# Attention's values multiplied by thirds of a group's rows, and placed by transfers on chip

## The reference

```python
h = jnp.concatenate([tok(x), txt], axis=1)          # 16 x 69 x 256
n = layernorm(h)
q, k, v = n @ wq.T, n @ wk.T, n @ wv.T              # q, k rotated
attn = softmax(einsum('bqd,bkd->bqk', qr, kr) / 16)
h = h + einsum('bqk,bkd->bqd', attn, v)
h = h + shared(n2) + routed_top2_of_8(n2)           # n2 = layernorm(h)
```

## Time and profile before

| | |
|---|---|
| median of 3 runs | 323.93 us (323.28 to 326.38) |
| the profiled execution | 324.18 us, of which the span is 322.0 us |
| busy: PE / DVE / ACT / POOL | 91% / 50% / 45% / 64% of the span |
| granted clock of TensorE, mean | 0.988 of full speed |
| chain that ended last | PE 51%, DVE 17%, DMA 10%, issue 8%, POOL 6%, ACT 4% |
| hardware queue of SP's DMAs (q1) | 14226 packets, 14.03 MB |

### The profile page before, as it was taken

How to read it: one execution, slowest core, us unless ns; L and a number is a source line. 1 busy time by engine, 2 the same in 40 slices (tenths; PEclk the granted TensorE clock), 3 DMA queues, 4 the chain that set the end, 5 groups by cost and what they waited for, 6 DMA issues and landing times.

```text
span 322.0 us, 6614 instructions
## 1 busy us (share of the span) xinstructions
PE 293.1 (91%) x2021; PEld 264.9 (82%) x2022; DVE 161.5 (50%) x414; ACT 144.6 (45%) x325; POOL 206.6 (64%) x168
## 2 busy tenths in 40 slices
PE   0899879898998999998999999999999999999970
PEld 0477878797898999986999989999899998999860
DVE  3777888988837998632233332333323333233220
ACT  3786332558779346524343333433334333343300
POOL 3466490546880007589889889888988897255541
PEclk9999999997999999999999999999999999999997
DMA  7996113024345233865433643632555432324432
GB/s 246 307 214 218 32 46 133 2 70 148 103 175 170 86 115 107 267 227 172 158 89 157 195 128 100 195 109 97 169 164 150 62 49 49 49 32 49 51 37 29
DMA packets 21988, 39.90 MB, mean 124 GB/s; under 512 B 2977, under 2 KB 18290, under 8 KB 19666
## 3 DMA queue, kind: packets, MB, share of 16 engines
q0 software_dynamic: 7456, 25.43, 29.6%
q1 hardware_dynamic: 14226, 14.03, 14.3%
q10 hardware_dynamic: 288, 0.20, 0.2%
HBM read 28.84 MB, written 6.93 MB: 111 GB/s over the span
## 4 chain that ended last, share of the span: by engine, by line
PE 51%; DVE 17%; DMA 10%; issue 8%; POOL 6%; ACT 4%; POOLq 2%; SPq 0%; DVEq 0%; ACTq 0%
PE ps L1007 11%; PE ps L1009 11%; PE ps L1008 11%; DMA out_tokens<-xy_all,dest 8%; PE ps L875 7%; PE ps L1055 4%; PE ps L906 2%; POOL out_tokens L611 2%; POOLq L608 1%; DVE ps L1299 1%; DVE qk L1298 1%; PE ps L977 1%; DVE hid L1415 1%; DMA xp<-in_patches 1%; ACT hn L737 1%
## 5 line engine op out<-in xcount | busy, mean ns | idle before, releaser
L456 POOL TENSOR_TENSOR ring<-stage,ring 128x512 fp32r<-128x512 f32 (+2 forms) x30 | 76.2, 2539 | 2.5
L1604 DVE TENSOR_TENSOR hgT<-ps,hgT 128x512 fp32r<-128x512 f32 x50 | 32.2, 686 | 72.3 <-ACT hgT L865 72.3
L1007 PE MATMUL ps<-ring,hgT 128*128 x200 | 58.2, 291 | 2.1 <-DVE xy_all L1610 1.5
L611 POOL DMA_INDIRECT out_tokens<-xy_all,dest x25 | 39.5, 1582 | 28.0 <-DMA out_tokens<-xy_all,dest 19.5
L1009 PE MATMUL ps<-ring,hgT 128*128 x200 | 56.2, 281 | 0.0
L1008 PE MATMUL ps<-ring,hgT 128*128 x200 | 56.1, 281 | 0.0
L857 ACT ACTIVATE hg<-ps 128x512 f32<-128x512 f32 x50 | 29.9, 598 | 47.7 <-PE ps L1009 47.7
L601 POOL DMA_INDIRECT xy_all<-normalized_tokens,dest x25 | 24.8, 991 | 31.7 <-DVE dest L1553 24.4
L1007 PE MATMUL ps<-ring,xgT 128*128 x100 | 41.5, 415 | 1.1 <-issue 0.6
L1007 PEld LDWEIGHTS ps<-ring,hgT 128*128 128x128 f32 x200 | 37.6, 188 | 2.6 <-issue 2.6
L1009 PE MATMUL ps<-ring,xgT 128*128 x100 | 39.4, 394 | 0.0
(11 more groups left out here) (200 smaller groups left out, 582.7 us busy)
## 6 DMA issues: line engine op xcount, KB each, us to landing
stage<-in_w_up POOLq DMA_DIRECT2D x9, 1024.0 KB, 5.5
stage<-in_w_dn POOLq DMA_DIRECT2D x9, 1024.0 KB, 5.6
xg<-xy_all SPq DMA_DIRECT2D x25, 128.0 KB, 2.1
xp<-in_patches SPq DMA_DIRECT2D x4, 384.0 KB, 7.3
normalized_tokens<-hn SPq DMA_DIRECT2D x4, 276.0 KB
residual_tokens<-h SPq DMA_DIRECT2D x4, 276.0 KB
ring<-in_tok_w SPq DMA_DIRECT2D x1, 768.0 KB, 6.6
base<-residual_tokens SPq DMA_DIRECT2D x3, 256.0 KB, 2.9
```

Source lines behind the costliest of these rows:

```text
L456: return nc.gpsimd.tensor_tensor(lo, stage[:, part, c0:c1], hi.bitcast(F32), ALU.subtract)
L611: pool.indirect_dma_start(out, bass.IndirectOffsetOnAxis(ap=dest[:, t:t + 1].bitcast(U32), axis=0), xy_all[:, t, :], None, compute_op=ALU. ...
L1007: nc.tensor.matmul(o, a[0], b[0], start=n == 0, stop=False)
L1604: v.tensor_tensor(hgT[:, c, 1, 4 * half:4 * half + 4, :], ps[:, turned_bank + half, :].rearrange("p (k t) -> p k t", k=4), hgT[:, c, 0, 4 ...
```

## The change

`attention_v` no longer goes by images of 69 rows but by thirds of a group, 92 rows each (`VROWS`): 18 matmuls instead of 24, thirds 0 and 1 in bank 6, third 2 in bank 7, and third 2 first. ACT copies the 92 x 768 result to a new tile `vrows`, of which there is one. The rows of an image now begin at partition 0, 69, 46 or 23 of some third, so SP moves them by DMAs from `vrows` to `vv`, six a group (`V_PIECES`), of 69, 23, 46, 46, 23 and 69 rows of 1 KB. `attention_out(g)` waits for all six; `attention_values(g)` waits for the six of the group before, since `vrows` is one buffer; and the wait of `attention_values` for `a_pv` goes over to SP. On SP, `place_values` of groups 0 and 1 stands ahead of `keep_normed(0)`, that of group 2 between `keep_normed(0)` and `keep_base(0)`, that of group 3 between `keep_normed(1)` and `keep_base(1)`.

```diff
+VTILES = 3
+VROWS = GT // VTILES
...
+        vrows = sb("vrows", [VROWS, VTILES, D], where=thirds)
...
+        V_PIECES, at = [], 0
+        while at < GT:
+            n = min(VROWS - at % VROWS, SEQ - at % SEQ)
+            V_PIECES.append((at // VROWS, at % VROWS, at // SEQ, at % SEQ, n))
+            at += n
...
-            for g in range(2):
-                keep_normed(g)
-                keep_base(g)
+            def place_values(g):
+
+                sp.wait_ge(a_vs, g + 1)
+                if g >= 2:
+                    sp.wait_ge(a_pv, g - 1)
+                for j, row, b, key, n in V_PIECES:
+                    sp.dma_start(vv[key:key + n, g % 2, b, :], vrows[row:row + n, j, :]).then_inc(v_in[g % 2], 16)
+
+            place_values(0)
+            place_values(1)
+            keep_normed(0)
+            place_values(2)
+            keep_base(0)
+            keep_normed(1)
+            place_values(3)
+            keep_base(1)
...
             def attention_values(g):
                 act.wait_ge(a_v, g + 1)
-                if g >= 2:
-                    act.wait_ge(a_pv, g - 1)
-                nc.scalar.activation(vv[:, g % 2, :, :].rearrange("p (a b) d -> p a (b d)", a=2),
-                                     ps[0:SEQ, 6:8, :], ACT.Copy).then_inc(a_vs, 1)
+                if g >= 1:
+                    act.wait_ge(v_in[(g - 1) % 2], 16 * len(V_PIECES) * ((g - 1) // 2 + 1))
+                nc.scalar.activation(vrows[:, :, :].rearrange("p j d -> p (j d)"),
+                                     ps[0:VROWS, 6:8, :].rearrange("p a c -> p (a c)")[:, 0:VTILES * D],
+                                     ACT.Copy).then_inc(a_vs, 1)
...
-                for b in (2, 3, 0, 1):
-                    if g >= 1 and b == 0:
+                for j in (2, 0, 1):
+                    if g >= 1 and j == 0:
                         te.wait_ge(a_pTs, g)
-                    last = split_product(ps[0:SEQ, 6 + b // 2, D * (b % 2):D * (b % 2 + 1)],
-                                         [([hT_n[:, v, c, GT * g + SEQ * b:GT * g + SEQ * (b + 1)] for v in range(2)],
+                    rows = slice(GT * g + VROWS * j, GT * g + VROWS * (j + 1))
+                    last = split_product(ps[0:VROWS, 6 + j // 2, D * (j % 2):D * (j % 2 + 1)],
+                                         [([hT_n[:, v, c, rows] for v in range(2)],
                                            [wv2[:, v, c, :] for v in range(2)]) for c in range(KD)])
                 last.then_inc(a_v, 1)
...
             def attention_out(g):
                 te.wait_ge(a_pTs, g + 1)
+                te.wait_ge(v_in[g % 2], 16 * len(V_PIECES) * (g // 2 + 1))
```

More of the change, by code:

```diff
@@ L182, in fusion_layer @@
         sb("slots12", [P, 4 * EW], where=early)
+        thirds = ExitStack()
+        vrows = sb("vrows", [VROWS, VTILES, D], where=thirds)
+        thirds.close()
         in_lane = sb("in_lane", [P, 2 * NT, P], F32R, where=early)
@@ L226, in fusion_layer @@
         img_in = [sem(f"img_in{i}") for i in range(NPT)]
+        v_in = [sem(f"v_in{n}") for n in range(2)]
         a_stats, a_rstd, a_normed, a_tr, a_hT = (sem(n) for n in ("a_stats", "a_rstd", "a_normed", "a_tr", "a_hT"))
```

## The result

The changed kernel takes 352.34 us in the median of 4 runs (349.9 to 353.43), the one before, run beside it, 325.03 (323.28 to 326.38). The ratio is 1.091, with a 95% interval of 1.082 to 1.100: 9% slower. The profiled execution took 353.43 us, 29.3 more than the one of before. Two runs further down, 354.06 us of the kernel with filler products and 327.67 of the kernel before with its stores cut, ran more than 1.5% above the fastest of their kernel at a lower granted clock, and are left out of the times there.

The account below looks back on a forecast made before the run. The prediction took the chain of waits through attention to bound the kernel, no engine's sum. The profiled 324.2 us plus 23.4 for PV of group 3's delay and 1.7 for the clock gave 349.3, so 349, range 330 to 355.

Parts of the forecast that it names:

- No gain from the products: PE in attention: six fewer products save 0.71 us a group, hidden in group 0 and slack in groups 2 and 3.
- The gains of at most 1.1 us: Attention: fewer products give at most 0.7 us, ACT's shorter copies in groups 2 and 3 0.4.
- 138 rows in a row on one engine: Transfers to vv: first engine carries 138 packets a group at 46 ns, 6.3 us, landing 7.1 us after first issue.
- A load of weights costs the queue 3.8 us: Hardware DMA queue: each 1 MB load by POOL that meets a busy queue costs it 3.8 us.
- Behind the stores, in order: SP's queue: pieces of groups 2 and 3 wait behind stores on the same engines, landing at 81.9 and 104.3.
- Group 1 hidden: PV of group 1: pieces land at 65.0, PV wants them at 67.0, so hidden by 2 us.
- The clock: PE after the idle times at PV of groups 0 and 3: half clock costs 1.7 us each.
- the last load of weights: Group 3's transfers: the load formerly at 85.65, now near 94.9, meets them and costs 3.8 us.
- Passed on whole: After attention: a delay of PV of group 3 goes through to the end whole, 23.4 us plus 1.7 for the clock.
- 23 rows do not spread: Rival, transfers: 23 and 46 rows go on 12 engines, still in order behind the stores; 333 us, chance 0.08.
- the transfers do not pass the stores: Rival, SP's queue: pieces pass the stores, only group 0's 5.1 + 1.7 us remain, less 0.4; 330.5 us, chance 0.08.
- nothing was in time but group 1: Rival, group 0: six pieces land within 5.1 us of first issue, all gains count; 323 us, chance 0.06.

Follow-up runs that it names:

- filler products: Changed kernel with unread products (58, 44 and 80) before PE's wait for the transfers of groups 0, 2 and 3; 345.1 us, ratio 1.061.
- kernels without transfers: Changed kernel with no transfers, PV reading two buffers of thirds where they lie, with 18 products or padded to 24; ratios 1.013 and 1.012.
- load later: Changed kernel with POOL's load of the second expert's up weights moved behind the first root; 343.79 us, ratio 1.063.
- spread: Changed kernel with every transfer cut in a multiple of 16 rows and a rest, 12 issues a group instead of 6; 343.59 us, ratio 1.060.
- thirds alone: Changed kernel without any transfer, PV reading two buffers of thirds where they lie (wrong rows); 330.85 us, ratio 1.013.
- padded thirds: Changed kernel without transfers, the last third multiplied twice to make 24 products a group; 328.51 us, ratio 1.012.
- the stores behind: Changed kernel with the transfers of groups 2 and 3 ahead of all four stores of groups 0 and 1 on SP; 351.47 us, ratio 1.076.
- the stores cut: Changed kernel in its own order, each store cut in 64 and 5 partitions; 343.98 us, ratio 1.063.

## Why the prediction was right

Forecast 349, measured 352.3. The mechanism held, and several terms were off in ways that cancelled, so that the number is closer than the working. Step by step:

- **No gain from the products.** Right, and stronger than said. The gains of at most 1.1 us didn't show in the kernels without transfers, which were 1.9 and 1.0 us later at the table. The prediction took the saving in group 0 as hidden. It was worse than hidden: behind the longer idle time the clock was at half (44.13 to 46.26 for the scores, 2.1 us instead of 1.2). It fell to half between 44 and 49 us in nine of the ten kernels with 18 products, and in none with 24.
- **138 rows in a row on one engine.** Right: 1.1 engines in use, two small packets in 48. With no load in the way group 0 took 9.0 us from issue to landing (load later), where 7.1 was forecast. A packet took 43 ns, not 46, so it is the rest that was too small: 9.0 less 138 packets of 43 ns is 3.1 us, not 0.8. Part of it is that two stores of zeros, issued at 44.9 and 45.3 us in that run, land near 47, and the forecast counted nothing ahead in the queue; what makes up the remainder stays open.
- **A load of weights costs the queue 3.8 us.** Measured 4.6. Together group 0's pieces landed at 59.8, not at 57.1.
- **Behind the stores, in order.** Right, by the two experiments that moved or cut the stores, 3.4 to 3.7 us for group 2 and 9 to 9.6 for group 3. PE was idle for 5.3 us before PV of group 2 (4.4 forecast).
- **Group 1 hidden.** Right.
- **The clock.** The mechanism was right, the size was not: 1.7 us was taken for each of two falls, by the one fall that the trace before showed. The rotation lost 3.8 us behind PV of group 0, and there was a fall at all three idle times.
- **What cancelled.** PV of group 2 started at 87.9 where 81.9 was forecast, 6.0 us late: 2.7 from group 0's landing, 2.1 from the clock, and some 1.2 in the queue from the store on. From there to PV of group 3 the forecast took 22.4 us, and it was 18.1. In its sum the last load of weights costs group 3's pieces 3.8 us. That load was issued at 102.22, and the hardware queue hardly slowed. From 102 to 104 and from 104 to 106 us:

```profile
q1 hardware_dynamic: 135, 0.14, 20.1%
...
q1 hardware_dynamic: 125, 0.12, 18.1%
```

At 72 packets a us it would have been 288 instead of 260: by the prediction's own measure the load cost 0.4 us. So PV of group 3 at 106.0, near the forecast's 104.3, is in part luck. The idle time before it shows the same: 8.9 us, where "over 10" was forecast.
- **Passed on whole.** Right: 25.1 us at PV of group 3, 29.2 at the end, the difference being half clock from 106 to 112 us (3 us) and about 1 us that stays open. The forecast had 1.7 us in that place.

The rivals fell as follows: 23 rows do not spread (56 to 58 us), the transfers do not pass the stores, and nothing was in time but group 1.

## What to carry to other kernels

Before a step is paid for with small DMAs, divide each one's rows by the engines that it will use, add up the rows on the first engine over everything in that queue (a store from 69 partitions used three of sixteen here), and set that against the time until someone waits. Count a saving on PE only if PE is on the path; where PE then idles, look at the granted clock behind the idle time, which may cost more than was saved. When a reordering changes nothing, look for the wait that has appeared elsewhere before dropping the theory: here cutting the stores kept the gain that moving them lost.

## What the hardware showed that was not expected

- The half clock lasts long after work resumes: 8.1 us at 0.50 behind 7.4 us of idle time, 7.1 behind 5.3, 6 behind 8.9. In the kernel before its one fall in attention was 4 us at 0.57 on average.
- There is no plain rule by the idle time before it: after 2.86 us (load later) PV ran at full speed, after 2.5 us the clock fell in nine kernels and not in a tenth (spread took 1.22 us for the same scores), with the thirds alone it was at half some 1.3 us after a wait of 1.53 us, and with the padded thirds about 1 us after one of 0.62.
- One issue on SP took 6.1 us (median of the 24 transfers 0.71), for group 3, while stores and transfers stood in the queue:

```profile
L416 SPq DMA_DIRECT2D vv<-vrows x24: 575/710/6112, 46.1 to 98.6; - x24
```

The six kernels that keep the uncut stores ahead of the transfers all have such an issue, of 3.6 to 7.1 us. With the stores behind none took more than 0.87 us, and with the stores cut none more than 1.52. Why it arises was not tried. In the changed kernel it wasn't the last wait: the sixth issue ended at 99.4, 6.6 us before PV. With the cut transfers (spread) it was 1.2 us before PV of group 3, so there the long issue may have cost time.
